# Empty semaphore instructions between the projection matmuls of a six-layer attention kernel

## The chip, the cores and the metric

The kernel runs on one core of a Trainium2 chip. The metric is the time on the device in microseconds (us), the median of several executions. Before the change it is 3812.87 us (three runs, 3811.61 to 3819.72). The execution that the profiler recorded took 3801.54 us; its span, from the first to the last instruction, is 3799.7 us, and the 1.8 us that are left lie around it.

## The reference

The input is x, 16 sequences of 256 tokens with 128 features, all float32. A first block adds windowed attention (window 64, 16 heads of 8) to x. Then follow six layers on a layer-normed x, and their result is added to x. It is this part that the change touches:

```python
def attn_layer(x, Wqkv, qs, ksc, Wo):                # x: 16 x 256 x 128
    q, k, v = split(x @ Wqkv, 3)                     # Wqkv: 128 x 3072, 16 heads of 64
    q = l2norm(q) * qs;  k = l2norm(k) * ksc
    q = rotary(q) * scale;  k = rotary(k) / scale
    out = local_attention(q, k, v)                   # window 32: own window and the one before
    return out @ Wo
for i in range(6):
    x = attn_layer(shift_tokens(x), Wqkv[i], q_scale[i], k_scale[i], Wo[i]) + x
    x = ffn_layer(shift_tokens(x), ln_g[i], ln_b[i], W1[i], b1[i], W2[i], b2[i]) + x
```

## The kernel before, in words

Each engine has its own instruction stream, written out by hand, and the streams meet only in semaphores. The first block (`stage1`) is a loop of 8 passes. The layers are cut in blocks of 128 tokens: 32 blocks per layer, 192 in all. One *step* `t` brings one new block in, and works on several older ones in the same step: block t gets its projections, block t-1 its transposes and scores, block t-3 its weighted values and its output projection, and so on. The function `steps` lays this out: 12 steps written out (`DRAIN`), then a loop of five laps (`Fori`) whose body is 32 steps written out, then the last 32 steps again written out, of which 20 still bring in a block.

TensorE (PE) runs `step_pe`. In each step its instructions stand in this order. A matmul is two instructions, a weight load and a multiply; a matmul of plain float32 is done in two passes and is four (the profile therefore counts twice as many of these as the code writes).

| part of a step | code | instructions |
|---|---|---|
| q projection, `project`, 6 matmuls 128x512 | L565 | 12 |
| Sx: 8 transposes of the softmax result | L575 | 16 |
| k projection | L582 | 12 |
| qk0: 8 transposes of q | L588 | 16 |
| AV: 64 float32 matmuls 64x32 (PT with VB, VA) | L605 | 256 |
| qk1: 8 transposes of k | L613 | 16 |
| v projection | L619 | 12 |
| even steps only: w1, 18 matmuls | L640 | 36 |
| odd steps only: xf, w2, f_xn | L652, L664, L674 | 4 + 12 + 4 |
| scores: 32 float32 matmuls 64x64 (kT with qT) | L691 | 128 |
| y: 8 float32 matmuls 128x128 (oT with wo_sb) | L703 | 32 |

With 29 semaphore and register instructions that is 1085 instructions for an even and an odd step together. One body of the loop has 17,369 (16 times 1085, and 9 more). `project` is called three times a step. Each call ends in a semaphore that starts ScalarE (`q_done`, `k_done`, `v_done`). `apart(e)` (L158) adds 1 to a semaphore, `waited`, on which nobody waits.

The other engines, by line: ACT squares q and k (L718, L726), copies the transposes (L721, L736, L746) and v (L753); DVE does the rotary embedding (L852, L856) and the sums; POOL adds and scales (L980, L959) and weighs the softmax (L991).

Of the kernel before, what the change touches and what calls it, by code (L numbers as in the profile page):

```python
# [22 lines left out]
INNER = HEADS * DH  # L23
# [48 lines left out]
def build(nc, x_in, w_first, wqkv, wo, qkscale, fw1, fw2, vectors, c_rot, c_small, out):  # L72
    ctx = ExitStack()
    with ctx:
# [3 lines left out]
        def sem(name):  # L78
            return ctx.enter_context(nc.semaphore(name))
# [71 lines left out]
        S = {n: sem(n) for n in (*STEP, *PER_SEQ, *LOADS, *PARTS, "xf0", "xf1", "vb0", "vb1", "vb2", "vb3", "phase", "loaded",  # L151
                                 "stored", "lane0", "lane1", "lane2", "lane3", "opened", "o_copied", "o_t", "o_sum", "zeroed",
                                 "cleared", "waited")}

        def apart(e):


            e.sem_inc(S["waited"], 1)  # L158
# [54 lines left out]
        def mm(out, lhsT, rhs, start=True, stop=True, **k):  # L213
            return T_.matmul(out, lhsT, rhs, start=start, stop=stop, **k)  # L214
# [279 lines left out]
        def blocks(pl, name, back, k):  # L494

            per = STEP[name]
            return pl.times(NBLOCKS * per) + ((pl.t - back) * per + k)

        def seqs(pl, name, q, k):

            per = PER_SEQ[name]
            return pl.times(SEQS * per) + (q * per + k)

        def layers(pl, per, ahead, k):

            return pl.times(per) + (ahead * per + k)
# [16 lines left out]
            for t in range(DRAIN, DRAIN + NBLOCKS):  # L523
                step(e, pl.at(t))

        def project(pair, high, low, first):
            for u in range(2):
                cols = slice(first + u * UNIT, first + (u + 1) * UNIT)
                out = pair[:, u * UNIT:(u + 1) * UNIT]
                mm(out, high, wq_h[:, cols], True, False)  # L530
                mm(out, low, wq_h[:, cols], False, False)
                last = mm(out, high, wq_l[:, cols], False, True)
            return last

        def projections(t):
            return (PA0, PA1) if t % 2 == 0 else (PA1, PA0)
# [8 lines left out]
        def step_pe(e, pl):  # L545
            t, b, then = pl.t, pl.t % BLOCKS, (pl.t - 1) % 2
            one, other = projections(t)
            bank0, bank1, bank2 = feed_banks(t)
            fresh = t % NBLOCKS == 0
            if pl.has(0):  # L550
                if b == 0:
                    e.wait_ge(S["xs_ready"], seqs(pl, "xs_ready", t // BLOCKS, 2))
                s = (t // BLOCKS) % 2
                high, low = (x[:, s, b * P:(b + 1) * P] for x in (xs_h, xs_l))
                if pl.has(1):
                    e.wait_ge(S["rotated"], blocks(pl, "rotated", 1, 2))
                if pl.seq(11) is not None:
                    e.wait_ge(S["gated"], seqs(pl, "gated", pl.seq(11), 2))
                if pl.seq(12) is not None:
                    e.wait_ge(S["x_done"], seqs(pl, "x_done", SEQS + pl.seq(12), 1))  # L560
                if pl.seq(10) is not None:
                    e.wait_ge(S["x_kept"], seqs(pl, "x_kept", pl.seq(10), 1))
                if fresh:
                    e.wait_ge(S["wq_low_q"], layers(pl, 1, t // NBLOCKS, 1))
                project(one, high, low, 0).then_inc(S["q_done"], 1)  # L565
            if pl.has(3):
                e.wait_ge(S["weighed"], blocks(pl, "weighed", 3, 1))
                if pl.has(4):
# [8 lines left out]
            if pl.has(0):  # L577
                if pl.has(1):
                    e.wait_ge(S["v_kept"], blocks(pl, "v_kept", 1, 1))
                if fresh:  # L580
                    e.wait_ge(S["wq_low_k"], layers(pl, 1, t // NBLOCKS, 1))
                project(other, high, low, INNER).then_inc(S["k_done"], 1)  # L582
            if pl.has(1):
                e.wait_ge(S["scaled"], blocks(pl, "scaled", 1, 1))
                if pl.has(3):
# [29 lines left out]
            if pl.has(0):  # L615
                e.wait_ge(S["rotated"], blocks(pl, "rotated", 0, 1))
                if fresh:
                    e.wait_ge(S["wq_low_v"], layers(pl, 1, t // NBLOCKS, 1))
                project(one, high, low, 2 * INNER).then_inc(S["v_done"], 1)  # L619

            q = pl.seq(10)
            if q is not None:
# [538 lines left out]
        @block.tensor  # L1161
        def _(pe):
            pe.wait_ge(S["loaded"], 64)
            stage1(pe, stage1_pe)
            meet(pe, 1)
            pe.wait_ge(S["cleared"], 1)
            steps(pe, step_pe)
            meet(pe, 2)
            finish(pe, "pe")
# [41 lines left out]
```

## Time and profile before

| | |
|---|---|
| median of 3 runs | 3812.87 us |
| profiled execution, its span | 3801.54 us, 3799.7 us |
| PE busy | 3233.2 us, 85% |
| DVE, ACT, POOL busy | 79%, 68%, 66% |
| mean granted TensorE clock | 0.933 |
| from start to 610 us | the first block, clock 0.70 |
| one lap of the loop (32 steps) | 523.6, 529.2, 523.5, 528.0, 526.0 us |

A PE that is 85% busy over the span is busier in the layers, since the first block waits much. "issue" is the profile's name for an engine that stands still with no semaphore wait to explain it. The queue named q8 brings blocks of instructions from memory, not data.

### The profile page before, as it was taken

The numbers are of one execution on the slowest core, as the hardware profiler recorded it, in microseconds if no ns is written. First come the engines' busy times: TensorE is split into PE (matmuls) and PEld (weight loads), VectorE is DVE, ScalarE is ACT, GpSimd is POOL, SyncE is SP. The second block draws the span as 40 slices with busy tenths as digits, with TensorE's granted clock in tenths as the row PEclk, the third lists the DMA queues.
The fourth block names the chain that finished last, engine by engine and source line by source line (L and its number), as shares of the span: only waits on it lengthen the run. The fifth ranks groups of instructions, "written<-read, shape, count | busy, mean of one in ns | idle before, by whom it ended". The sixth has DMA issues, their size and how long they took to land.

```text
span 3799.7 us, 126632 instructions
## 1 busy us (share of the span) xinstructions
PE 3233.2 (85%) x52674; PEld 2775.9 (73%) x52674; DVE 3009.8 (79%) x4462; ACT 2600.9 (68%) x3787; POOL 2503.0 (66%) x2289
## 2 busy tenths in 40 slices
PE   3444447999989999989999899999899998999996
PEld 2333236788878888778888788888788887888885
DVE  5766767888888788888788887888887888888883
ACT  2222235777777778778787777787687777788775
POOL 1000007887777778778787777887787787788772
PEclk8666668999999999999999999999999999999997
DMA  1000001111111111111111111111111111111111
GB/s 57 0 0 0 0 0 35 37 55 33 33 34 39 57 35 36 36 35 38 57 36 35 30 41 59 36 35 36 34 38 53 36 36 35 37 37 40 30 35 32
DMA packets 54638, 129.97 MB, mean 34 GB/s; under 512 B 10944, under 2 KB 28864, under 8 KB 53312
## 3 DMA queue, kind: packets, MB, share of 16 engines
q1 hardware_dynamic: 54080, 122.02, 11.0%
q8 instruction: 413, 6.77, 0.7%
q14 instruction: 145, 1.19, 0.1%
HBM read 19.25 MB, written 2.10 MB: 6 GB/s over the span
## 4 chain that ended last, share of the span: by engine, by line
PE 56%; DVE 17%; issue 11%; ACT 11%; POOL 5%; DMA 0%; SPq 0%; POOLq 0%; ACTq 0%; DVEq 0%
PE pair L214 44%; PE pair L217 12%; ACT qT L736 6%; POOL qk L959 3%; DVE ss L860 2%; DVE ts L856 2%; DVE pair L873 1%; DVE den L908 1%; ACT sq L726 1%; DVE qk L852 1%; ACT sq L718 1%; POOL Sx L991 1%; DVE qT L359 1%; DVE mx L877 1%; DVE VA L344 0%
## 5 line engine op out<-in xcount | busy, mean ns | idle before, releaser
L980 POOL TENSOR_TENSOR qk<-qk,ts 128x1024 f32<-128x1024 f32 x384 | 910.9, 2383 | 218.8 <-DVE ts L856 205.0
L959 POOL TENSOR_TENSOR qk<-qk,rn 128x1024 f32<-128x1024 f32 x384 | 734.0, 1932 | 43.6 <-issue 28.8
L852 DVE TENSOR_TENSOR qk<-pair,tab 128x1024 f32<-128x1024 f32 x384 | 468.7, 1221 | 370.3 <-ACT sq L718 368.2
L214 PE MATMUL pair<-wq_h,xs_h 128*128 128x512 f32 x1154 | 515.7, 447 | 36.5 <-issue 18.6
L217 PE MATMUL pair<-small,qk 128*128 128x128 f32 x3192 | 452.4, 285 | 79.0 <-ACT qT L736 40.4
L217 PEld LDWEIGHTS pair<-small,qk 128*128 128x128 f32 x3192 | 360.2, 145 | 168.4 <-issue 96.0
L991 POOL TENSOR_TENSOR Sx<-Sx,rden 128x1024 f32<-128x1024 f32 x192 | 365.7, 1905 | 157.3 <-DVE rden L911 157.3
L856 DVE TENSOR_TENSOR ts<-pair,tab 128x1024 f32<-128x1024 f32 x384 | 466.7, 1215 | 0.0
L214 PE MATMUL pair<-wq_h,xs_l 128*128 128x512 f32 x1152 | 465.0, 404 | 0.0
L860 DVE TENSOR_REDUCE ss<-sq 128x16 f32<-128x1024 f32 x384 | 464.6, 1210 | 0.0
L713 ACT ACTIVATE Sx<-Sx 128x1024 f32<-128x1024 f32 x192 | 203.7, 1061 | 378.0 <-DVE Sx L881 378.0
L214 PE MATMUL pair<-wq_l,xs_h 128*128 128x512 f32 x1152 | 460.9, 400 | 0.0
L214 PE MATMUL pair<-PT,VB 64*64 64x32 f32 x12288 | 384.0, 220 | 28.7 <-issue 26.3
L214 PE MATMUL pair<-PT,VA 64*64 64x32 f32 x12288 | 381.8, 219 | 24.9 <-issue 24.9
L214 PE MATMUL pair<-kT,qT 128*64 128x64 f32 x12288 | 400.9, 224 | 2.0 <-DVE pair L873 1.9
L214 PEld LDWEIGHTS pair<-kT,qT 128*64 128x64 f32 x12288 | 374.6, 138 | 35.8 <-issue 35.8
L736 ACT ACTIVATE qT<-pair 64x1024 f32<-64x1024 f32 x384 | 391.2, 1019 | 11.3 <-PE pair L217 6.5
L214 PE MATMUL pair<-oT,wo_sb 128*128 128x128 f32 x3072 | 394.4, 282 | 0.0
L214 PEld LDWEIGHTS pair<-PT,VB 64*64 64x64 f32 x12288 | 332.4, 134 | 62.7 <-issue 62.7
L214 PEld LDWEIGHTS pair<-oT,wo_sb 128*128 128x128 f32 x3072 | 358.1, 192 | 12.9
L214 PEld LDWEIGHTS pair<-PT,VA 64*64 64x64 f32 x12288 | 335.0, 135 | 27.8 <-issue 27.8
L375 POOL TENSOR_TENSOR VA<-X,w_raw 128x128 f32<-128x128 f32 x8 | 3.6, 454 | 523.6 <-PE pair L214 523.6
(201 smaller groups left out, 7079.4 us busy)
## 6 DMA issues: line engine op xcount, KB each, us to landing
VB<-VA SPq DMA_DIRECT2D x192, 384.0 KB, 3.5
VB<-VA SPq DMA_DIRECT2D x96, 128.0 KB, 3.5
wq_raw<-wqkv SPq DMA_DIRECT2D x6, 1536.0 KB, 8.4
xf<-xT SPq DMA_DIRECT2D x96, 64.0 KB, 1.9
xf<-xT SPq DMA_DIRECT2D x96, 63.8 KB, 2.0
wo_sb<-wo SPq DMA_DIRECT2D x6, 512.0 KB, 3.7
out<-X SPq DMA_DIRECT2D x8, 256.0 KB, 2.3
w_raw<-fw SPq DMA_DIRECT2D x6, 341.0 KB, 8.3
```

Source lines behind the costliest of these rows:

```text
L214: return T_.matmul(out, lhsT, rhs, start=start, stop=stop, **k)
L217: return T_.transpose(out, in_, ident if idn is None else idn)
L359: V_.tensor_reduce(L.rsum, h3(L.p, W1N), axis=AX.X, op=ALU.add).then_inc(L.done, 1)
L713: A_.activation(rows, rows, ACT.Exp).then_inc(S["exp_done"], 1)
L718: A_.activation(sq[:, 0, :], one[:, :], ACT.Square).then_inc(S["squared"], 1)
L736: last = A_.activation(qT[rows, :, :, odd * WIN:(odd + 1) * WIN], PC[rows, :].rearrange("p (a w q) -> p a w q", a=PAIRS, w=4), ACT.Copy)
L852: V_.tensor_tensor(h3(qk[:, now, kind, :], DH), h3(source[:, :], DH), rep(tab[:, 2 * kind, b, :], HEADS, DH), ALU.mult)
L856: V_.tensor_tensor(ts[:, kind, :].rearrange("p (h a c) -> p h a c", **halves), swapped, sines, ALU.mult).then_inc(S["rotated"], 1)
L860: V_.tensor_reduce(ss[:, kind * HEADS:(kind + 1) * HEADS], h3(sq[:, kind, :], DH), axis=AX.X, op=ALU.add).then_inc(S["summed"], 1)
L959: G_.tensor_tensor(x, x, bc(rn[:, then, kind * HEADS:(kind + 1) * HEADS], HEADS, DH), ALU.mult).then_inc(S["scaled"], 1)
L980: G_.tensor_tensor(qk[:, now, kind, :], qk[:, now, kind, :], ts[:, kind, :], ALU.add).then_inc(S["added"], 1)
L991: G_.tensor_tensor(x, x, bc(rden[:, now, :], HEADS, KEYS), ALU.mult).then_inc(S["weighed"], 1)
```

## The change

`fill(e, t, j)` puts empty `apart` instructions behind the matmuls of `project`: in even steps 26 for the 18 projection matmuls (two behind each of the first 8, one behind each other), in odd steps 41 (three behind each of the first 5, two behind each other). They go in wherever a step brings in a block. Two steps have 1085 + 67 = 1152 instructions then, the body of the loop 17,369 + 16 x 67 = 18,441, and the 12 steps ahead of the loop 6 x 67 = 402 more. Nothing else moves: every other instruction of every engine keeps its place among the others, and a listing of the built programs that leaves semaphore instructions out reads the same for both but for the line numbers.

```diff
+        FILL = ((1, 8), (2, 5))
+
+        def fill(e, t, j):
+
+            each, more = FILL[t % 2]
+            for _ in range(each + (j < more)):
+                apart(e)
+
-        def project(pair, high, low, first):
+        def project(e, t, pair, high, low, first):
             for u in range(2):
                 cols = slice(first + u * UNIT, first + (u + 1) * UNIT)
                 out = pair[:, u * UNIT:(u + 1) * UNIT]
+                j = first // INNER * 6 + u * 3
                 mm(out, high, wq_h[:, cols], True, False)
+                fill(e, t, j)
                 mm(out, low, wq_h[:, cols], False, False)
+                fill(e, t, j + 1)
                 last = mm(out, high, wq_l[:, cols], False, True)
+                if u == 0:
+                    fill(e, t, j + 2)
             return last
...
-                project(one, high, low, 0).then_inc(S["q_done"], 1)
+                project(e, t, one, high, low, 0).then_inc(S["q_done"], 1)
+                fill(e, t, 5)
...
-                project(other, high, low, INNER).then_inc(S["k_done"], 1)
+                project(e, t, other, high, low, INNER).then_inc(S["k_done"], 1)
+                fill(e, t, 11)
...
-                project(one, high, low, 2 * INNER).then_inc(S["v_done"], 1)
+                project(e, t, one, high, low, 2 * INNER).then_inc(S["v_done"], 1)
+                fill(e, t, 17)
```

## Rows read from the trace of the kernel before

**Rows 1.** The page: span, PE's busy lines, the clock, the instruction queue.
```profile
span 3799.7 us, 126632 instructions
PE 3233.2 (85%) x52674; PEld 2775.9 (73%) x52674; DVE 3009.8 (79%) x4462; ACT 2600.9 (68%) x3787; POOL 2503.0 (66%) x2289
q8 instruction: 413, 6.77, 0.7%
```

**Rows 2.** PE's waits, whole span: line, releaser, us in total, times, longest.
```profile
PE pair L214 <- issue: 69.7, 53, 5.7
PE pair L217 <- issue: 11.1, 14, 1.3
```

**Rows 3.** Timeline of PE, undisturbed steps: start, length, what, count, [idle before].
```profile
1417.45 2.05 PE L214 MATMUL pair<-oT,wo_sb 128*128 128x128 f32 x16
1426.89 1.06 PE L217 MATMUL pair<-small,qk 128*128 128x128 f32 x8 [0.23 <-ACT qT L736]
1433.44 2.05 PE L214 MATMUL pair<-oT,wo_sb 128*128 128x128 f32 x16
1448.55 2.05 PE L214 MATMUL pair<-oT,wo_sb 128*128 128x128 f32 x16
```

**Rows 4.** Timeline of PE, two steps with a gap inside AV.
```profile
1510.87 2.05 PE L214 MATMUL pair<-oT,wo_sb 128*128 128x128 f32 x16
...
1517.93 0.32 PE L214 MATMUL pair<-PT,VB 64*64 64x32 f32 x8
...
1520.93 0.30 PE L214 MATMUL pair<-PT,VA 64*64 64x32 f32 x4 [0.95 <-issue]
1521.16 1.09 PE L217 MATMUL pair<-small,qk 128*128 128x128 f32 x8
...
1527.74 2.05 PE L214 MATMUL pair<-oT,wo_sb 128*128 128x128 f32 x16
...
1537.70 0.26 PE L214 MATMUL pair<-PT,VA 64*64 64x32 f32 x4 [1.53 <-issue]
...
1544.36 2.05 PE L214 MATMUL pair<-oT,wo_sb 128*128 128x128 f32 x16
```

**Rows 5.** DMA queues from 1518 to 1519 us: packets, MB, share.
```profile
q8 instruction: 1, 0.02, 7.9%
```

**Rows 6.** The same from 1406 to 1407 us.
```profile
q8 instruction: 1, 0.02, 7.8%
```

**Rows 7.** Timeline of PE: AV of an odd step without a gap.
```profile
1408.99 0.32 PE L214 MATMUL pair<-PT,VB 64*64 64x32 f32 x8
...
1411.29 0.41 PE L217 MATMUL pair<-small,qk 128*128 128x128 f32 x2 [0.23 <-ACT qT L736]
```

**Rows 8.** Timeline of PE: a gap between AV and qk1.
```profile
1661.55 1.09 PE L217 MATMUL pair<-small,qk 128*128 128x128 f32 x8 [1.28 <-issue]
```

**Rows 9.** Windows: us, busy (x instructions) of PE, PEld, DVE, ACT, POOL, PEclk, DMA.
```profile
1392.00:1393.80 1.80, 0.52 (x35) 0.41 (x27) 1.80 (x3) 0.73 (x1) 1.35 (x1) 1.00 0.00 0
1393.80:1397.20 3.40, 3.38 (x21) 3.12 (x22) 2.20 (x3) 1.89 (x2) 2.37 (x1) 0.52 0.02 5
1811.40:2334.90 523.50, 491.37 (x8449) 428.94 (x8450) 438.55 (x552) 406.80 (x550) 413.05 (x371) 0.99 0.14 40
```

**Rows 10.** Timeline of PE at the end of a lap.
```profile
1282.04 2.05 PE L214 MATMUL pair<-oT,wo_sb 128*128 128x128 f32 x16
1289.78 0.79 PE L214 MATMUL pair<-wq_h,xs_h 128*128 128x512 f32 x1 [5.69 <-issue]
```

**Rows 11.** PE's sequencer by line, 1509.5 to 1512 us: ns each, first and last start.
```profile
L556 PEldq EVENT_SEMAPHORE  x1: 51/51/51, 1511.0 to 1511.0; - x1
L560 PEldq ALU_OP  x1: 32/32/32, 1511.1 to 1511.1; - x1
L562 PEldq EVENT_SEMAPHORE  x1: 51/51/51, 1511.2 to 1511.2; - x1
```

**Rows 12.** The same, 1527 to 1534 us.
```profile
L558 PEldq ALU_OP  x1: 32/32/32, 1527.8 to 1527.8; - x1
L569 PEldq EVENT_SEMAPHORE  x1: 51/51/51, 1530.6 to 1530.6; - x1
L586 PEldq EVENT_SEMAPHORE  x1: 51/51/51, 1533.3 to 1533.3; - x1
```

**Rows 13.** Timeline of PE: projection matmuls.
```profile
1512.99 0.39 PE L214 MATMUL pair<-wq_h,xs_l 128*128 128x512 f32 x1
1513.23 0.40 PE L214 MATMUL pair<-wq_l,xs_h 128*128 128x512 f32 x1
```

## Prediction

> **What bounds the kernel now.** I read the page first, then the waits of PE, then PE's timeline step by step, then the queue of instruction blocks beside it. PE is the busiest engine [rows 1]. In undisturbed steps it hardly rests: from one y part to the next pass 15.99 us (an even step) and 15.11 us (an odd one), 31.1 us for two, and the one gap in AV's neighbourhood is 0.23 us in front of qk1 [rows 3]. The granted clock there is full. So whatever holds PE up lengthens the step. The waits show what does: 67 times, 80.8 us in all, PE stood still for "issue", that is for no semaphore [rows 2]. The timeline shows where. In the steps that end with the y parts at 1527.74 and 1544.36, PE stops inside AV, for 0.95 and 1.53 us, and the steps take 16.87 and 16.62 us, 0.9 and 1.5 us more than their undisturbed kind [rows 3, 4].
>
> These gaps lie at a fixed distance in PE's program. The first is in front of the last 8 instructions of its AV (four matmuls are left, [rows 4]); the second one has 211 of AV's 256 behind it. Between them lie, by the table of parts and with the semaphore instructions, 8 + 16 + 12 + 36 + 128 + 32, then 12 + 16 + 12 + 16 + 211, and 13 control instructions: 512, twice 256. All gaps of AV lie on multiples of 256 from each other. The instruction queue agrees: 413 packets of 6.77 MB are 16.4 KB each [rows 1], and the 105,348 matmul halves with some 2,800 control instructions, less the 3,500 that the first loop repeats without a new packet, are about 254 for each packet. So PE's program comes in blocks of 256, and a gap is PE waiting for its next block. One packet starts between 1518 and 1519 us, and the gap ends at 1520.93; that is 2 to 3 us later [rows 4, 5].
>
> **When a block comes late.** AV is 256 instructions that PE runs in 1.9 us (two steps' worth: 1408.99 to about 1411 [rows 7]), so each AV holds exactly one boundary, and if the packet for it starts only inside AV, its 2 to 3 us don't fit. Call p the place of the boundary in AV. I placed all boundaries of the 192 steps in the built program and looked for the gap at each. p up to 170: 130 cases, no gap. p from 171 to 210: 23 cases, 13 gaps. p from 211 to 262 (the last six are already in qk1, as in [rows 8]): 47 cases, 44 gaps, 1.16 us on average. The middle group tells the mechanism. A packet for a boundary can start once PE's sequencer has passed the boundary before it. In the step of [rows 7] (odd, p = 202) that one lies in the q projection; the packet started at 1406 to 1407, ahead of AV [rows 6], and there was no gap. In other laps the same place missed. After q the sequencer stands at L569 (in the odd step of [rows 12] from about 1527.9 to 1530.6), then, after a short burst, at L586 until 1533.3. A boundary that it passes just before such a wait gets its packet only after the wait, one with some 0.4 us of sequencer work behind it gets it at once: that fits all groups, but I infer it.
>
> **The change part by part.**
> 1. Empty instructions on PE itself: 67 for two steps. They are the sequencer's work, not the array's: existing ones take 51 ns and follow each other every 0.1 us, and they run at 1511.0 to 1511.2 while PE still has y matmuls to do from 1510.87 on [rows 4, 11]. At 0.105 us each they are 7.0 us for two steps; bounds are 0, if all lie beside matmuls, and 7.0 x 96 = 675 us, if none does. Behind a 512-column matmul (0.24 us apart, [rows 13]) three take 0.32 us, two 0.21. The cover: ahead of q lies y, 1.8 us, and behind q the sequencer waits 2.7 us at L569 [rows 12] and has 1.8 us of fill to do; ahead of k lie the Sx transposes, 0.85 us, and two per matmul don't use them up; ahead of v lies qk1, 0.85 us. I take 0. If the lead in front of q were gone, five matmuls in an odd step would each lose 0.08 us: 0.4 x 96 = 38 us.
> 2. Where the boundaries fall. 402 instructions more ahead of the loop and 1152 for two steps put them, in every lap, at p = 255 (t = 12, 16, ... 40, even), 183 (the odd step after), 127 and 56 or a few less, and again: four steps are nine blocks. p = 127 and 56 never had a gap. p = 255 has the boundary before it in the last instruction of qk0; at p = 250 the trace had a gap in all five laps, [rows 4] is one: 0.9 us per step. p = 183 is in the middle group, with the boundary before it in the q projection of an odd step, at its 17th instruction of 30. Behind it stand eight fills, 0.8 us of sequencer work before L569, more than enough by the inference above. I take no gap; the other end is a gap as in [rows 4], 1.5 us, or 1.6 with the clock counted (below).
> 3. The loop. Before: with the undisturbed step lengths taken off, gaps cost the five laps 51 us, 10.3 each (the third lap took 523.5 us, [rows 9]). After: 8 x 0.9 = 7. Saved 5 x 3.3 = 16.
> 4. The 12 steps ahead of the loop: before, six gaps at p = 225 to 233, one of which halved the clock, 8 us in all. After, one boundary stands at the first instructions of qk1, 1.1 us; the others are early or have fills behind the boundary before them. Saved 6.
> 5. The last 32 steps: before nine gaps, 10 us. After, some three (p = 254, 234, 250): 3 to 5 us. Saved 5.
> 6. The clock. Gaps of 1.3 us and more sometimes cost twice: after the gap that ends at 1393.80 the granted clock was 0.52 for 3.4 us, which is the lower level of 1.2 GHz, and it had been 1.00 before [rows 9]. That step took 2.9 us extra. Gaps of 1.1 us never did this. These costs are inside the sums of 3 to 5.
> 7. The jump back, four times: 5.69 us of idle PE [rows 10]. The new body starts elsewhere in its block; I take no change, ends -2 and +2 us each, -8 to +8.
> 8. Twenty-five more packets and 6432 updates of a semaphore nobody waits for: the instruction queue is 0.7% busy [rows 1]; nothing.
>
> Sum: -16 - 6 - 5 = -27 us. The profiled execution took 3801.5 us, so 3774.5; it lay 11.3 us under the median of the runs, so on their scale 3812.9 - 27 = 3786.
>
> The Trainium skill, "Runtime: NRT & Kernel Launch", section "Instruction fetch mechanics", says the same of the size, blocks of 256 instructions; the trace agrees, at about 254 per packet. It also says that the cost of crossing a block is mostly hidden, because the sequencer issues slower than blocks arrive. By that rule parts 2 to 5 are zero and the time stays at 3813. The gaps of 0.95, 1.53 and 1.28 us [rows 4, 8] speak against it in AV.
>
> **The rivals.**
> - *The odd steps stop too* (slower). The place is p = 183, the price 1.6 us for each of 8 steps in a lap, 5 laps: 64 us; 3786 + 64 = 3850. It decides from about four in ten of these steps missing: then 26 us are lost and the gain is gone. For it: p = 202 in an odd step missed in two of five laps, p = 177 too, p = 197 in all. Against it: in none of these did the sequencer have fills to work through before its wait.
> - *Gaps only change place.* Some of the steps at p = 183 miss, three to five in ten, and the sum of gaps is as before: 3786 + 25 = 3811. The skill's rule leads to the same time in another way, with no gaps worth counting. For it: the middle group was mixed. Against it: with fixed places every lap should do the same.
> - *The fills are not covered.* The sequencer's lead in front of q or k is shorter than I read it, and PE starves behind threefold fills: up to 38 us, less the 27: 3824. Against it: the waits at L569 and L586 [rows 12].
> - *More goes than I count.* Fills also bring the packets for p = 255 forward, and 34 us (5 x 7) more go: 3752. Against it: no fill stands between qk0 and AV.
>
> **How the numbers follow.** Forecast 0.56 (3772 to 3800), odd steps stop 0.12, change of place 0.17, fills not covered 0.10, more goes 0.05. What a measurement can tell from no change is 0.2%, 7.6 us. Faster: 0.55 of the forecast, 0.05 of the last and 0.02 of the third, 0.62. Within: 0.01, 0.10 of the third and 0.02 of the fourth, 0.13. Slower: 0.12, 0.05 and 0.08, 0.25. The range 3766 to 3836 leaves out 0.05 below, and most of the 0.12 and a little of the 0.10 above. The forecast's own range is 3772 to 3800.
>
> **What the profile of the changed kernel would show.** Right: PE's "issue" waits fall from 67 to about 55, of at most 1.3 us but for the jumps; in a lap every fourth step (even) has a gap of 1.0 to 1.1 us in front of qk1 or in AV's last instructions, every odd step is clean at 15.1 us, and the clock stays at 1.00 through the laps but for the change of layer. Wrong: gaps in the odd steps at three quarters of AV (rival one); q, k or v matmuls more than 0.24 us apart (rival three); a packet that starts before AV in the steps with p = 255 (the last); gaps at other places than these (my count of the boundaries is off).

## The result and the profile after

The changed kernel took 3763.68 us, median of 4 runs (3760.97 to 3766.94), beside 3812.24 us (3801.94 to 3819.72) for the kernel before: ratio 0.9875, interval 0.985 to 0.990. The forecast was 3786, so the sign was right, the gain was 49 us and not 27, and the time lies 2 us under the range.

The page of the profiled execution (3762.11 us), the lines that answer to [rows 1]: span; busy time of the engines; packets, MB and share of the instruction queue.

```profile
span 3760.3 us, 133064 instructions
PE 3225.0 (86%) x52674; PEld 2764.3 (74%) x52674; DVE 3007.5 (80%) x4462; ACT 2599.8 (69%) x3787; POOL 2500.1 (66%) x2289
...
q8 instruction: 441, 7.23, 0.8%
```

The same matmuls, 6432 instructions more, and 28 packets more. PE's waits for no semaphore, the lines that answer to [rows 2]: us in total, times, longest.

```profile
PE pair L214 <- issue: 42.9, 44, 4.5
PE pair L217 <- issue: 5.1, 5, 1.3
```

80.8 us in 67 waits became 48.0 us in 49. That is 33 of the 39 us by which the profiled execution got shorter (3801.5 to 3762.1). PE's busy time fell by 8.2 us [rows 1]. That fits the clock: in the 151 steps of the loop's row below, 3.4 us ran at the granted clock of 0.50 and not 20.5.

PE's timeline of an even and an odd step after (start, us, engine and line, tiles, count, idle before and what ended it), for [rows 3, 4, 7]:

```profile
1408.42 0.29 PE L214 MATMUL pair<-PT,VA 64*64 64x32 f32 x6
1409.27 0.30 PE L214 MATMUL pair<-PT,VA 64*64 64x32 f32 x2 [0.56 <-issue]
1409.50 1.09 PE L217 MATMUL pair<-small,qk 128*128 128x128 f32 x8
...
1416.08 2.05 PE L214 MATMUL pair<-oT,wo_sb 128*128 128x128 f32 x16
...
1424.51 0.30 PE L214 MATMUL pair<-PT,VA 64*64 64x32 f32 x8
1425.04 1.06 PE L217 MATMUL pair<-small,qk 128*128 128x128 f32 x8 [0.23 <-ACT qT L752]
```

The even step still stops, two of the profile's matmuls ahead of AV's end, where p = 255 was to be. The odd step has only its 0.23 us in front of qk1, as an undisturbed one has. The packet for the even step's block starts as its AV does (1406.65); the one for the odd step's starts 4 us ahead of its AV (1422.74). The instruction queue from 1406 to 1407 us, and from 1418 to 1419:

```profile
q8 instruction: 1, 0.02, 6.8%
```
```profile
q8 instruction: 1, 0.02, 7.3%
```

By region, summed over the steps (from the last y matmul of one to that of the next) of the two profiled executions:

| | before | after | difference |
|---|---|---|---|
| up to the first y part | 635.9 | 636.1 | +0.2 |
| steps ahead of the loop | 124.4 (6 gaps) | 118.9 (2, one in front of qk1) | -5.5 |
| loop, 151 steps without t = 12 of laps 2 to 5 and t = 32 | 2396.8 (41 gaps, 52.5 us) | 2370.0 (31, 27.7 us) | -26.8 |
| loop, change of layer (t = 32) | 143.0 | 142.3 | -0.7 |
| loop, step behind the jump back | 90.5 | 90.6 | +0.1 |
| last steps | 354.8 | 348.1 | -6.7 |

### The profile page after: what moved, and what is told of

It is laid out like the page before. It is cut to its first block, busy times and chain, and to the rows that moved or that the text cites. A ratio compares the mean times of both kernels' runs of the same rounds, so it can differ in the third digit from the quotient of the medians.

```text
span 3760.3 us, 133064 instructions
## 1 busy us (share of the span) xinstructions
PE 3225.0 (86%) x52674; PEld 2764.3 (74%) x52674; DVE 3007.5 (80%) x4462; ACT 2599.8 (69%) x3787; POOL 2500.1 (66%) x2289
## 4 chain that ended last, share of the span: by engine, by line
PE 50%; DVE 21%; issue 12%; ACT 10%; POOL 6%; DMA 0%; POOLq 0%; SPq 0%; DVEq 0%; ACTq 0%
PE pair L214 40%; PE pair L217 10%; ACT qT L752 5%; DVE ts L872 4%; DVE ss L876 3%; POOL qk L975 3%; DVE qk L868 2%; DVE pair L889 2%; DVE den L924 2%; ACT sq L734 2%; POOL Sx L1007 1%; ACT sq L742 1%; DVE qT L359 1%; DVE mx L893 1%; DVE Sx L897 1%
## 5 line engine op out<-in xcount | busy, mean ns | idle before, releaser
L214 PE MATMUL pair<-PT,VB 64*64 64x32 f32 x12288 | 375.4, 220 | 4.4 <-ACT PT L737 2.4
```

## The experiments

Each ran beside the kernel before on the same chip; its times there had medians of 3797 to 3802 us. A "gap", in the table above and from here on, is a distance of over 0.3 us from the start of one matmul to the start of the next inside AV; for the kernel before, the five stops in front of qk1 at t = 34 (like the one of [rows 8]) are counted with them. Its length is that distance. Unless something else is said, gaps are counted in the 151 steps of the loop. p is the boundary's place in AV as in the prediction. A "fill" or "empty" is one `apart` instruction. The lines PEldq are PE's sequencer; the traces show it at work on the program ahead of the matmuls, and how far ahead is called its lead.

**The two kernels again.** No edit.

> The kernel before, unchanged, for a second profile of it. Theory (the gaps of PE at block boundaries are partly a matter of luck, since packets in the mixed group of places sometimes start too late and long gaps sometimes halve the clock): ratio 1.00, and the profiled execution has 55 to 70 gaps of over 0.3 us in AV or ahead of qk1, not at the same steps in all laps, and lies anywhere from 3800 to 3820 us. Rival (the executions differ by something else, as transfers or the first block): the same gaps at the same steps as in the first profile, to within two or three, and the difference elsewhere.

Before: 3801.99 us (3794.44 to 3811.02, 10 runs), ratio 1.000 (0.9985 to 1.0014), with 44 gaps of 55.1 us together.

> The changed kernel, unchanged, beside the others of this group. Ratio 0.985 to 0.990 against before, as measured. Theory (its gaps stand at fixed places and are short): its runs spread less than those of the kernel before, within 8 us, and 40 gaps of 0.5 to 1.5 us stand at the same steps. Rival (the gain is of one execution): ratio nearer 0.993, the sum of the terms.

After: 3756.38 us (3749.49 to 3762.51, 5 runs), ratio 0.988 (0.9863 to 0.9897), 31 gaps of 22.5 us. The gain and the number of gaps repeat; the runs spread over 13 us, not within the 8 that I expected.

**Another place for the same period: 40 empties ahead of all.**

```diff
+            for _ in range(40):
+                apart(pe)
```

> The changed kernel with 40 empty instructions more at the very start of PE's stream, where PE waits for the first loads anyway (4 us of cover over 10 us of waiting). They move all block boundaries of the layers 40 instructions back in AV: from p = 255, 183, 127, 56 to 215, 143, 87, 16. Theory (with fills in q and k, a boundary in q or k gets its successor's packet in time, so only p of about 235 to 262 makes a gap): no gaps in AV at all, 3764 less about 30 to 37, so 3727 to 3734. Rival (the place p alone decides, as read from the kernel before, where 44 of 47 boundaries with p from 211 to 262 had a gap): every fourth step has a gap of 1.2 to 1.4 us instead of 1.0, 3764 to 3785.

3758.26 us (3753.24 to 3759.72), ratio 0.9889 (0.9873 to 0.9906). AV's gaps went, one was left of 31, and the time did not follow: it is that of the changed kernel. Small stops of 0.1 to 0.6 us came elsewhere. In 22 steps PE stops for 0.4 us in front of qk1 and not for 0.23. Where a boundary lies at p = 16 of an odd step, the next one is in front of xf (two v matmuls, then xf):

```profile
1332.47 0.47 PE L214 MATMUL pair<-wq_h,xs_l 128*128 128x512 f32 x1
1332.77 0.46 PE L214 MATMUL pair<-wq_l,xs_h 128*128 128x512 f32 x1
1333.40 0.41 PE L217 MATMUL pair<-small,xf 128*128 128x128 f32 x2 [0.16 <-issue]
```

From the matmul before to xf 0.63 us pass (0.23 in the changed kernel). The v matmuls in front of it start 0.30 us apart and not 0.23, the pace of two fills (0.151 us each, shown below): in this step the fills are not covered. Such a step took 15.3 to 16.1 us, not 15.1. The expectation (3727 to 3734) missed: I had counted the boundaries in AV alone.

**No fixed places: one empty less per matmul, 1145 for two steps.**

```diff
-        FILL = ((1, 8), (2, 5))
+        FILL = ((1, 4), (2, 2))
```

> FILL = ((1, 4), (2, 2)): 60 fills for two steps instead of 67, so 1145 instructions, and the boundaries drift by 7 a pair through all places of AV. Theory (fills make the packets early, and only p of 235 to 262 is bad): 27 of the 192 boundaries are there, 0.6 to 0.9 us each, 16 to 24 us in all against some 37 us in the changed kernel: 3744 to 3752. Rival (the fixed places are what helps, and a drift brings the old gaps back): as the kernel before, 3800 to 3815.

3761.32 us (3760.2 to 3769.74), ratio 0.9906 (0.989 to 0.9923), 20 gaps of 17.0 us, and five stops of 0.7 to 1.1 us in front of qk1 at t = 21. Places that drift by seven a pair gain nearly as much. So a whole number of blocks isn't what helps. The time lies between the two that were expected.

**The same places, the fills elsewhere.** In odd steps no fills behind q and k; the 29 stand behind w1 of the even step.

```diff
+            if t % 2 == 1 and j < 12:
+                return
...
+            if t % 2 == 0 and pl.has(0):
+                for _ in range(29):
+                    apart(e)
```

> The changed kernel with the same 1152 instructions and the same places p of all boundaries in AV, but the 29 fills of q and k in odd steps stand behind the w1 matmuls of the even step before (18 matmuls and 128 score matmul halves cover 3.0 us of them). The boundary ahead of p = 183 now lies in y's later half, with hardly any sequencer work behind it before the wait at L569, as p = 177 to 189 had it in the kernel before (5 gaps in 10). Theory (sequencer work behind the boundary decides): a third to two thirds of the odd steps with p = 183 get a gap of 1.0 to 1.3 us, 3764 plus 20 to 50. Rival (the place in AV decides, or the odd steps are safe as such): no new gaps, 3762 to 3768.

4036.88 us (4033.77 to 4044.09), ratio 1.063 (1.0612 to 1.0648). All 80 odd steps of the loop stayed clean, the 40 with p at or near 183 among them, with no fills behind q or k. A third to two thirds of them were expected to stop. So the eight q fills aren't needed for that, and my inference has no support here. It is not a clean test: PE came late to every odd step. What cost 6% was PE starved behind the pile. Its timeline and the sequencer's fills there (count, ns each, first and last start):

```profile
1417.89 0.28 PE L214 MATMUL pair<-f_l,w_h 128*85 128x256 f32 x1
1420.46 0.74 PE L214 MATMUL pair<-kT,qT 128*64 128x64 f32 x18 [2.29 <-issue]
```
```profile
L158 PEldq EVENT_SEMAPHORE  x30: 51/51/51, 1415.9 to 1420.3; - x30
```

The 30 `apart` take 4.4 us, 0.151 us from one to the next (29 of them are the fills). The gap is 2.3 us of that; the other 2 us are, as an estimate, the lead that the sequencer had on w1.

**A third place: 28 empties ahead of all.** As the 40 above; p = 227, 155, 99, 28.

> The changed kernel with 28 empty instructions at the start of PE's stream: boundaries at p = 227, 155, 99, 28 (225, 152, 96, 25 in the second half of a lap), so neither in the last 25 instructions of AV nor at the end of qk1. Theory (a boundary needs sequencer work behind the one before it; at 227 the one before it stands in k, with four to six fills behind): hardly a gap in the laps, neither in AV nor ahead of xf: ratio 0.980 to 0.984. Rival (227 is too late, as it was in the kernel before, where p of 223 to 229 always had a gap): the same time as the changed kernel or up to 10 us more, with a gap of 1.1 to 1.4 us at every fourth step.

3774.98 us (3767.45 to 3778.52), ratio 0.9928 (0.9912 to 0.9943). The boundary at p = 227 stopped PE in 20 of 20 steps; its packet starts in AV:

```profile
1408.43 0.30 PE L214 MATMUL pair<-PT,VA 64*64 64x32 f32 x8
1409.60 0.32 PE L214 MATMUL pair<-PT,VB 64*64 64x32 f32 x8 [0.86 <-issue]
```

Four fills of k stood behind the boundary that precedes it. At p = 223 (t = 36) six did, and 5 of 5 were clean; at p = 225 (t = 40), six also, 5 of 5 stopped. I had expected hardly a gap; four fills are not enough.

**Fills at one projection only.** Two behind each k matmul, or each v, or each q: 24 for two steps, 1109 in all.

```diff
-            each, more = FILL[t % 2]
-            for _ in range(each + (j < more)):
+            for _ in range(2 if 6 <= j < 12 else 0):
```

(`j >= 12` for v, `j < 6` for q.)

> Fills only behind the six k matmuls, two each, in every step: 24 for two steps. The period of 1109 puts boundaries in turn at p of about 266, 218, 181, 132, 96, 47. Theory (work between q's end and the wait at L586 lets the packet start): no gaps at 218 and 181, some small ones at 266; ratio 0.984 to 0.991. Rival (only place and period count): the place is as bad as in the kernel before, 10 of 32 steps with gaps of 1.0 to 1.5 us, ratio 0.998 to 1.006.

k: 3752.55 us (3752.33 to 3762.96), ratio 0.9881 (0.9862 to 0.9901), 4 gaps left. p = 218 of odd steps, where the kernel before always stopped near by, was clean.

> The same number of fills, 24 for two steps, all behind the six v matmuls: boundaries at p of about 230, 193, 144, 108, 60, 23. Theory: no fill stands between the boundaries that precede these and the waits in front of AV, so 230 always and 193 more often than not make a gap, 8 to 10 a lap; ratio 0.997 to 1.005. Rival (any fill helps, by slowing the sequencer down anywhere): ratio 0.985 to 0.992 as with the k fills.

v: 3777.74 us (3774.66 to 3783.42), ratio 0.9936 (0.9919 to 0.9953), 31 gaps of 34.1 us, 30 of them in the 30 steps with p = 228 to 233. The time lies between the two expected, and p had moved too. So v once more with 12 empties ahead of all, which puts its boundaries at k's places; and q, which has them there by itself.

> Two empties behind each v matmul, none behind q and k (24 for two steps, 1109 instructions), and twelve empties at PE's start, so that the boundaries lie at the same places in AV as in the kernel with empties behind k alone: in a lap about 266, 218 (odd steps t = 13, 19, 25, 31, 37, 43), 181, 132, 95 and 46. The only difference is what lies between a boundary and the sequencer's next stop: here no fills of k stand behind the boundary ahead of p = 218. Theory (the fills behind k keep the sequencer moving, so the packet is asked for before the stop): a gap of 0.9 to 1.4 us at 218 in all six steps of every lap, as before.py had it, some 35 us more than the kernel with k fills: 3780 to 3790, ratio 0.994 to 0.998. Rival (the place alone, or its distance, decides, not the fills): 218 is clean as there, 3750 to 3762, ratio 0.988.

> Two empties behind each q matmul, none behind k and v (24 for two steps, 1109 instructions); the places in AV are again about 266, 218 (odd), 181, 132, 95, 46. The q fills stand ahead of the boundary that precedes p = 218, so they can't bring its packet forward. Theory (only fills behind that boundary count): gaps of 0.9 to 1.4 us at 218 in all six steps of every lap, 3780 to 3790, ratio 0.994 to 0.998. Rival (any fills of the step give the sequencer a slower, steadier pace, wherever they stand): 218 clean, 3750 to 3762, ratio 0.988.

> Empties behind the k matmuls alone once more, two each, beside the others on one chip. Theory: 3752 plus or minus 5, ratio 0.988, the same as the changed kernel within 0.2% or a shade under it, and 25 to 35 us under the two kernels with the same places in AV but their fills behind v or q. Rival (the 3752 of the first run was luck of the session): no difference from those two.

| fills behind | time, us | ratio | gaps at p = 216 to 221 |
|---|---|---|---|
| k, again | 3751.23 (3750.5 to 3758.44) | 0.9879 (0.9861 to 0.9897) | 3 of 30 (4 of 30 the first time) |
| q | 3775.72 (3763.95 to 3776.66) | 0.9931 (0.9907 to 0.9955) | 18 of 30 |
| v | 3793.56 (3785.58 to 3805.96) | 0.9991 (0.9977 to 1.0005) | 30 of 30 |

Same places, same number of instructions, one chip: 42 us between k and v, and v is no faster than the kernel before. The place alone doesn't decide; what stands behind the boundary ahead of it does. PE's timeline of the same step (t = 19 of the second lap), k first (its first run, on another chip):

```profile
1386.62 0.32 PE L214 MATMUL pair<-PT,VB 64*64 64x32 f32 x8
...
1388.39 0.30 PE L214 MATMUL pair<-PT,VA 64*64 64x32 f32 x8
1388.92 1.06 PE L217 MATMUL pair<-small,qk 128*128 128x128 f32 x8 [0.23 <-ACT qT L751]
```

and v:

```profile
1396.55 0.32 PE L214 MATMUL pair<-PT,VB 64*64 64x32 f32 x8
...
1398.09 0.28 PE L214 MATMUL pair<-PT,VA 64*64 64x32 f32 x3
1399.29 0.25 PE L214 MATMUL pair<-PT,VA 64*64 64x32 f32 x3 [0.92 <-issue]
```

The sequencer's lines ahead of them (L592 is the wait in front of k, L600 the one in front of qk0, L158 the fills), and then the instruction queue. With k fills, the packet between 1384.2 and 1385.2 us:

```profile
L592 PEldq ALU_OP  x1: 32/32/32, 1383.0 to 1383.0; - x1
L158 PEldq EVENT_SEMAPHORE  x12: 51/51/51, 1383.1 to 1385.0; - x12
L600 PEldq EVENT_SEMAPHORE  x1: 51/51/51, 1385.5 to 1385.5; - x1
```
```profile
q8 instruction: 1, 0.02, 9.3%
```

With v fills, the packet between 1396.4 and 1397.4 us:

```profile
L592 PEldq ALU_OP  x1: 32/32/32, 1392.9 to 1392.9; - x1
L600 PEldq EVENT_SEMAPHORE  x1: 51/51/51, 1395.5 to 1395.5; - x1
```
```profile
q8 instruction: 1, 0.02, 6.0%
```

With k fills the sequencer works on for 1.9 us behind the boundary, the packet starts in that time (1384.72), and that is 1.9 us ahead of AV. Without them it runs into L600 at once and stands till 1395.5, and the packet starts at 1396.92, 0.4 us into AV. The boundary ahead isn't at the same place in the two: 256 instructions back lie the Sx transposes with v fills, and k with k fills, since the fills count. The sequencer passes both before the wait L600, the one with v fills earlier. That q lies between is not explained, and its expectation (30 gaps, 3780 to 3790) missed: twelve of its packets started 2.6 us ahead of AV, while the sequencer stood, eighteen after it.

**The same 67 fills by a table**, so that a boundary with p near 219 has ten of k behind the one ahead of it; 28 empties ahead of all.

```diff
-        FILL = ((1, 8), (2, 5))
+        FILL = ((3, 3, 3, 2, 2, 2, 3, 2, 2, 2, 2, 2, 1, 1, 1, 1, 1, 1),
+                (3, 3, 3, 3, 3, 2, 3, 2, 2, 2, 2, 2, 1, 0, 1, 0, 1, 0))
...
-            each, more = FILL[t % 2]
-            for _ in range(each + (j < more)):
+            for _ in range(FILL[t % 2][j]):
```

> The same 67 empties in two steps as in the changed kernel, but by a table: two or three behind each q and k matmul, one or none behind v; and 28 empties at PE's start. Boundaries in a lap at p = 219 (even), 146 (odd), 91 (even), 19 (odd). Theory (p = 219 has about eight fills of k, 1.2 us of sequencer work, behind the boundary before it, where the kernel with p = 227 had four and missed in each lap): 219 clean in all laps, nothing left in AV, laps about 2355 and the whole 3750 to 3758, ratio 0.986 to 0.989. Rival (219 stops whatever stands behind the boundary before it): six gaps of 1.2 us a lap, as in the kernel with p = 227: 3770 to 3778, ratio 0.992.

3739.19 us (3731.26 to 3744.97, 5 runs), ratio 0.9844 (0.9824 to 0.9864), 2 gaps of 31 left in the 151 steps, which took 2349.3 us. It is the fastest, and faster than I expected (3750 to 3758): every run of it is under every run of the kernel with k fills beside it, and under those of the changed kernel in its two sessions. Its span, its waits, and its fourth lap, from q to q (us, busy of each engine, clock, DMA), then the same lap of the changed kernel and of the one before:

```profile
span 3736.6 us, 133092 instructions
```
```profile
PE pair L214 <- issue: 19.2, 13, 5.3
PE pair L217 <- issue: 5.2, 6, 1.3
```
```profile
2304.55:2820.50 515.95, 491.47 (x8449) 427.85 (x8449) 438.46 (x551) 406.48 (x548) 412.84 (x370) 0.99 0.14 40
```
```profile
2317.54:2838.49 520.95, 492.87 (x8448) 429.72 (x8449) 438.79 (x551) 406.66 (x548) 412.58 (x370) 0.99 0.14 40
```
```profile
2341.90:2868.67 526.77, 495.44 (x8448) 433.26 (x8449) 438.11 (x549) 406.53 (x548) 413.20 (x370) 0.98 0.14 39
```

Taken over all kernels, a boundary at p = 205 to 232 by the number of fills behind the boundary ahead of it (steps of the loop but t = 12 and 32): none, 93 of 105 with a gap (75 of 75 but for the q kernel); four, 20 of 20; six, 7 of 20; eight or more, 10 of 125. The packet's start tells these 270 steps apart better than the fills do. In the 140 without a gap it lies 0.4 to 2.8 us ahead of AV's first matmul; in the 130 with one, between 0.15 us ahead and 0.9 us behind, but for one (0.84 us ahead, a gap of 0.36 us). The gap ends 2.2 to 2.9 us after the packet's start.

## Why the prediction was wrong, step by step

The sum missed by 22 us: 12 in the gaps, most of them in step 3, and 10 in carrying the profiled execution over to the median.

- *What bounds the kernel, and where boundaries fall* (the first paragraphs and step 2): right. All gaps of the loop lie in AV's last eight instructions, in even steps, as placed; all 80 odd steps of the loop are clean at 15.1 us. There are 49 issue waits, 55 were forecast.
- *Step 1, fills cost nothing*: right for these numbers. Undisturbed pairs of steps still take 31.1 us. But a fill takes 0.151 us and not the 0.105 that I took from [rows 11], where rows of other instructions stood; two of them (0.30 us) are more than a projection matmul (0.23), and the cover is the sequencer's lead, which the pile of 29 and the stops of the kernel with 40 empties used up.
- *Step 3, the loop*: this is the term that failed, in its size. I forecast 16 us saved, with 8 gaps of 0.9 us a lap left, 40 in all. 26.8 were saved: 31 gaps were left that count. None came at t = 32. There PE has the lower clock behind a wait of 8.9 us (below), the sequencer passes the wait in front of qk0 1.6 to 2.7 us ahead of AV and not 1.1, and the packet starts 0.6 to 1.7 us ahead of AV. At t = 12 of the laps behind a jump a gap came, but the wait at the jump got shorter by as much (the four steps cost +0.1 together). These nine gaps are some 8 us. Undisturbed, the 151 steps would take 71 x 15.99 + 80 x 15.11 = 2344.1 us, so the 31 gaps cost 25.9 us, 0.84 each and not 0.9, which is 2 us; and the kernel before had lost 52.7 us in these steps and not 51. One reason for the lower price is that a gap this late takes the place of the 0.23 us in front of qk1. The wait at t = 32 stands in front of the Sx transposes and is ended by DVE's xT; this line has PE's waits for it from 1256 us on, and four of the nine are of 8.9 us:

```profile
PE pair L217 <- DVE xT L901: 37.5, 9, 8.9
```

- *Step 4 and 5, ahead of the loop and the last steps*: right, 5.5 for 6 and 6.7 for 5. *Step 7, the jump*: right, +0.1 for four. *Step 8*: right, with 28 packets more and not 25.
- *From the profiled execution to the median*: wrong as well. I carried over that the profiled execution of before lay 11.3 us under its median. After lay 1.6 under its own, and the changed kernel's second profiled execution 5.4 us above (3761.8 beside a median of 3756.4). It was scatter, and part of it lay in the median: in the later sessions the kernel before had medians of 3801.9, 3800.7 and 3797.2, so 3812.9, of three runs, was high and the profiled 3801.5 was not low. So the profiled sum was 27 forecast and 39 found (12 of the miss of 22), and some 10 are this.
- *Why p = 183 is clean* (the inference in "When a block comes late"): the step was clean, the reason isn't shown. Without fills behind the boundary ahead of it it was clean too. The same reason is shown at another place: at p = 216 to 221 the fills behind a boundary in k decide.
- *The rivals*: the odd steps don't stop; the gaps that changed place are fewer; the fills are covered. "More goes than I count" (3752; its 5 x 7 is 35 and not 34) came nearest to the time, but not the way: the packets for p = 255 (t = 12 and 32 aside) still start from 0.03 us ahead of AV's start to 0.5 us after it.
- *The clock, step 6*: "Gaps of 1.1 us never did this" doesn't hold. In lap 2, the step t = 28 has a gap of 1.06 us from one AV matmul to the next (0.84 us of idle time by the profile). Behind it the granted clock was 0.50 for 3.4 us, the lower of the two levels, 1.2 GHz, and the projection matmuls start 0.43 us apart, about half of the full rate; the step took 18.42 us. From 1531.0 to 1535.4 us, up to the gap's end, the granted clock had been 1.00.

```profile
1535.16 0.30 PE L214 MATMUL pair<-PT,VA 64*64 64x32 f32 x2 [0.84 <-issue]
...
1537.54 0.63 PE L214 MATMUL pair<-wq_h,xs_l 128*128 128x512 f32 x1
1537.96 0.63 PE L214 MATMUL pair<-wq_l,xs_h 128*128 128x512 f32 x1
1538.39 0.63 PE L214 MATMUL pair<-wq_h,xs_h 128*128 128x512 f32 x1
```

The Trainium skill's rule that crossing a block is mostly hidden ("Runtime: NRT & Kernel Launch", section "Instruction fetch mechanics") would have put the time at 3813. The runs of this kernel don't agree with it: with the boundaries at the same places in AV, the kernel with v fills has 30 gaps at them and takes 3794 us, the one with k fills has 3 and takes 3751.

## What to carry to other kernels

An engine that streams short instructions can stand still for its own program: look for "issue" waits at a fixed distance in its stream, and for the instruction queue's packet ahead of each, which here started at least 0.4 us before the fast stretch where there was no gap, and about with it or inside it where there was one. Some 1.2 us or more of small sequencer work (eight fills or more) behind the boundary before that one went with no gap in 115 of 125 steps and cost nothing, as long as it fitted in the sequencer's lead. Where the boundaries fall mattered as well: with the same 67 fills, the kernels with 0, 28 and 40 empties ahead had ratios of 0.988, 0.993 and 0.989 to the kernel before, and the one with the table 0.984. And when a few tenths of a per cent count, one profiled execution's distance from the median is scatter and isn't carried over.

## What the runs showed that I had not expected

- Empty semaphore additions on PE follow each other every 0.151 us though each shows 51 ns, so one takes three times what I would have read from its duration.
- Where the sequencer stood at the wait in front of qk0, the packet started 1.4 to 1.9 us after it moved on, in all 30 steps of the last kernel with v fills (L600 at 1395.45 and the packet at 1396.92 in the one shown). Where it had fills to work through, the packet mostly came while it worked, but not at a fixed distance from the boundary: with k fills 1.5 us in the step shown (1383.2 to 1384.72), and 1.2 to 3.4 us in the 20 steps of that run whose boundary lies on a fill. Why it varies is open. The q kernel's early packets are an exception that stays open.
- A gap of 1.06 us between two matmul starts was once followed by 3.4 us at half clock; of the other gaps of that length or more in the 151 steps of the changed kernel none was.
- 24 empties, all behind k, do as much as the change's 67 (3751 to 3753 us beside 3756 to 3764), and the same 24 behind v, with the boundaries at the same places, do nothing (3794 us, ratio 0.9991).
